# The opening of a two-layer decoder kernel: queues of the first loads, preparation of batches 0 and 1, places of the context projections

## The reference

```python
# x: (8, 256, 128), ctx_1024: (8, 256, 128), all fp32
x = x + self_attention_16_heads(layernorm(x))            # layer 0, heads of 8 columns, W_qkv, W_out
x = x + attention_1_head(layernorm(x), ctx_1024)         # layer 0, keys and values from the context
x = x + expert_mlp(layernorm(x))                         # layer 0
x = x + causal_attention_1_head(layernorm(x))            # layer 1
x = x + attention_16_heads(layernorm(x), ctx_1024)       # layer 1
x = x + light_and_routed_heavy_mlp(layernorm(x))         # layer 1, top 128 of 256 tokens
```

## Time and profile before

| | |
|---|---|
| median of the runs | 435.55 us |
| the profiled execution | 432.98 us |
| its span in the profile | 431.2 us |
| busy: TensorE, VectorE, ScalarE, GpSimd | 357.8, 323.7, 262.1, 141.9 us |

### The profile page before, as it was taken

The page is one execution under the profiler, slowest core; times in us unless marked ns, Lnnn a source line. Parts: engine busy times, 40 slices in busy tenths (PEclk is TensorE's granted clock), DMA queues, the critical chain, the costliest instruction groups (busy, mean ns, idle before and its releaser), DMA issues.

```text
span 431.2 us, 9413 instructions
## 1 busy us (share of the span) xinstructions
PE 357.8 (83%) x3164; PEld 208.3 (48%) x3164; DVE 323.7 (75%) x929; ACT 262.1 (61%) x582; POOL 141.9 (33%) x223
## 2 busy tenths in 40 slices
PE   2454899999999969599987589999989888769793
PEld 1342544454544348469976423444444443326583
DVE  5331888999899346725795687989999994489996
ACT  2130688888888835566554306887878788655531
POOL 3550555446400001301233432456654222221111
PEclk9985999999999997999998956999999999969987
DMA  6213124222360000000000231221221100000003
GB/s 193 74 51 98 45 73 110 76 64 57 106 179 3 2 0 2 2 2 0 2 0 2 74 100 48 51 64 46 70 64 45 45 2 3 0 0 2 0 2 97
DMA packets 36260, 19.98 MB, mean 46 GB/s; under 512 B 4038, under 2 KB 35318, under 8 KB 36214
## 3 DMA queue, kind: packets, MB, share of 16 engines
q1 hardware_dynamic: 35894, 19.25, 16.7%
q10 hardware_dynamic: 320, 0.13, 0.1%
HBM read 5.58 MB, written 1.05 MB: 15 GB/s over the span
## 4 chain that ended last, share of the span: by engine, by line
PE 43%; DVE 33%; ACT 7%; issue 6%; POOL 5%; SPq 3%; DMA 2%; DVEq 0%; ACTq 0%; POOLq 0%
DVE negmax_sb L785 13%; PE pv_ps L1188 10%; PE s_ps L1142 9%; DVE late_sb L1015 5%; PE prep_ps L1098 3%; SPq L405 3%; ACT probT_sb L521 3%; PE s_ps L1238 3%; PE prep_ps L1102 2%; PE s_ps L1151 2%; PE out_ps L1270 2%; POOL rstd_sb L445 2%; PE s_ps L1287 2%; DVE xn_sb L762 2%; PE s_ps L1253 1%
## 5 line engine op out<-in xcount | busy, mean ns | idle before, releaser
L785 DVE TENSOR_REDUCE negmax_sb<-s_ps 128x2 bf16<-128x512 f32 x256 | 162.4, 688 | 35.9 <-PE s_ps L1151 35.8
L521 ACT ACTIVATE probT_sb<-s_ps 128x512 f32<-128x512 f32 x256 | 142.2, 597 | 29.9 <-PE s_ps L1142 27.8
L1151 PE MATMUL s_ps<-stack_sb 62*128 62x256 bf16 x512 | 93.6, 288 | 3.5 <-DMA stack_sb<-parts_sb 3.1
L1142 PE MATMUL s_ps<-stack_sb 63*128 63x256 bf16 x512 | 90.3, 276 | 7.1 <-ACT probT_sb L521 3.2
L1188 PE MATMUL pv_ps<-probT_sb,v_aug_sb 128*32 128x256 f32 x1024 | 69.4, 389 | 0.8 <-ACT probT_sb L521 0.8
L1142 PEld LDWEIGHTS s_ps<-stack_sb 63*128 63x128 bf16 x512 | 30.3, 94 | 65.6 <-ACT probT_sb L521 40.3
L443 POOL TENSOR_SCALAR rstd_sb<-mv_sb 128x2 f32<-128x2 f32 x32 | 7.1, 222 | 124.6 <-DVE mv_sb L754 124.5
L543 ACT ACTIVATE qkf_sb<-prep_ps,b_qkv_sb 128x256 f32<-128x256 f32 x56 | 23.9, 470 | 26.7 <-PE prep_ps L1102 19.7
L1188 PEld LDWEIGHTS pv_ps<-probT_sb,v_aug_sb 128*32 128x32 f32 x1024 | 26.9, 110 | 25.8 <-issue 13.7
L1151 PEld LDWEIGHTS s_ps<-stack_sb 62*128 62x128 bf16 x512 | 30.6, 96 | 11.6 <-DVE negmax_sb L785 6.4
L845 DVE SCALAR_TENSOR_TENSOR x_all_sb<-out_ps,den_inv_sb,x_all_sb 128x128 f32<-128x128 f32 x32 | 9.8, 346 | 25.1 <-PE out_ps L1270 24.9
(11 more groups left out here) (177 smaller groups left out, 659.6 us busy)
## 6 DMA issues: line engine op xcount, KB each, us to landing
stack_sb<-parts_sb SPq DMA_DIRECT2D x192, 64.0 KB, 2.1
x_all_sb<-x SPq DMA_DIRECT2D x4, 256.0 KB, 3.5
ctxT_sb<-ctxT SPq DMA_DIRECT2D x2, 512.0 KB, 5.0
f_w_sb<-f_w SPq DMA_DIRECT2D x2, 512.0 KB, 4.0
out<-x_all_sb SPq DMA_DIRECT2D x4, 256.0 KB, 2.4
d_w_sb<-d_w SPq DMA_DIRECT2D x2, 320.0 KB, 3.6
w_att_sb<-w_att SPq DMA_DIRECT2D x2, 256.0 KB, 3.8
b_vo_sb<-b_vo SPq DMA_DIRECT2D x1, 512.0 KB, 4.9
```

What stands on the lines that cost most here:

```text
L521: act.activation(probT[:, c % 8], s2_ps[c % 2][:, :, :], ACT.Exp, scale=DH ** -0.5).then_inc(exp_ready, 1)
L785: dve.tensor_reduce(negmax[:, n % 2, :, max_column(max_head(h))], s1_ps[c % 3][:, :, :], axis=AX.X, op=ALU.max, negate=True).then_inc(max_ ...
L1142: i = pe.matmul(s2_ps[c % 2][:, k, :], stack[rows, s3, 1, h // 2, k * P:(k + 1) * P], stack[rows, s3, 0, h // 2, :], start=True, stop=True)
L1151: i = pe.matmul(s1_ps[c % 3][:, k, :], stack[rows, s3, 0, hp, k * P:(k + 1) * P], stack[rows, s3, 1, hp, :], start=True, stop=True)
```

## The change

- ScalarE's queue issues both halves of the context, behind a wait for the first quarter of x. SyncE's queue has neither.
- `b_vo` is loaded in two parts: its first layer early, under `w_in`; the other three after the stack fills, under a semaphore of their own, on which GpSimd's first `v_ctx_bias` waits. The second `w_att` and the second quarter of x come ahead of the fills, and all three fills stand before the stack of batch 0.
- Layer norm of batch 1 is computed beside that of batch 0 in step -3, and GpSimd clears stacks 1 and 2 right after their two `rstd_step_`.
- The six key copies of batch 0 are issued on GpSimd's queue (`load_first_keys`), under a semaphore of their own; SyncE issues the six query copies. Who waits for the stack of batch 0 waits for both.
- The split of batch 1 is done by VectorE, at head 9 of step -2 (`FIRST`).
- Of the context projections three run at head 15 of step -2 and five in step -1, after heads 1, 4, 7, 10 and 13.

```diff
@@ -62,9 +62,9 @@
 TOP = 80.0
 LN2 = float(np.log(2.0))
 
-KV_AT = {-2: (8, 14), -1: (0, 2, 4, 10, 12, 14)}
-
-FIRST = (0, B)
+KV_AT = {-2: (15, 15, 15), -1: (1, 4, 7, 10, 13)}
+
+FIRST = (0, 1, B)
 
 UP_AT = (2, 5, 8, 12, 14)
 AHEAD = 2
@@ -207,7 +207,7 @@
         prep_bf = prep_ps[:, :, :].bitcast(bf16)
 
         x_in = [sem(f"x_in{i}") for i in range(4)]
-        w_in, w_cross_in, w_rest_in = sem("w_in"), sem("w_cross_in"), sem("w_rest_in")
+        w_in, w_cross_in, w_rest_in, b_rest_in = sem("w_in"), sem("w_cross_in"), sem("w_rest_in"), sem("b_rest_in")
         ctx_in = [sem(f"ctx_in{i}") for i in range(2)]
         kv_psum, kv_copied, v_ctx_ready = sem("kv_psum"), sem("kv_copied"), sem("v_ctx_ready")
         ones_ready, stack_clear = sem("ones_ready"), sem("stack_clear")
@@ -219,7 +219,7 @@
         part1_ready, rest_ready, parts_ready = sem("part1_ready"), sem("rest_ready"), sem("parts_ready")
         v_psum, v_ready = sem("v_psum"), sem("v_ready")
         bv_ready, fold_psum, bias_folded = sem("bv_ready"), sem("fold_psum"), sem("bias_folded")
-        stacked = [sem(f"stacked{i}") for i in range(3)]
+        stacked, first_keys = [sem(f"stacked{i}") for i in range(3)], sem("first_keys")
         s1_psum, max_ready, maxT_psum, maxT_ready = sem("s1_psum"), sem("max_ready"), sem("maxT_psum"), sem("maxT_ready")
         max_in = [[sem(f"max_in{i}{hf}") for hf in range(2)] for i in range(3)]
         s2_psum, exp_ready, pv_psum, uT_ready = sem("s2_psum"), sem("exp_ready"), sem("pv_psum"), sem("uT_ready")
@@ -254,6 +254,12 @@
         block = ctx.enter_context(nc.Block())
         MANY = (0, B)
 
+        def wait_stacked(eng, n):
+
+            if n == 0:
+                eng.wait_ge(first_keys, STACKED // 2)
+            eng.wait_ge(stacked[n % 3], STACKED * (n // 3 + 1) - (STACKED // 2 if n % 3 == 0 else 0))
+
         def has(n, lo):
 
             return lo <= n < lo + B
@@ -336,7 +342,7 @@
             if m >= 1:
                 eng.wait_ge(parts_ready, m)
             if m >= 2:
-                eng.wait_ge(stacked[(m - 2) % 3], STACKED * ((m - 2) // 3 + 1))
+                wait_stacked(eng, m - 2)
             eng.tensor_copy(parts[:, u, :, 0, :], qkf[:, u]).then_inc(part1_ready, 1)
             eng.wait_ge(part1_ready, n + 1)
             eng.tensor_tensor(rest[:, :, :], qkf[:, u], parts[:, u, :, 0, :], ALU.subtract).then_inc(rest_ready, 1)
@@ -352,32 +358,30 @@
                 sp.dma_start(x_all[:, tiles, :], t["x"].rearrange("b (t p) d -> p (b t) d", p=P)[:, tiles, :]).then_inc(x_in[c], 16)
 
 
+            def load_b_vo(ls, landed):
+                sp.dma_start(b_vo[:, ls, :, :].rearrange("p l w d -> p (l w d)"),
+                             t["b_vo"][ls].rearrange("l w d -> (l w d)").partition_broadcast(P)).then_inc(landed, 16)
+
             load_x(0)
             sp.dma_start(w_att[:, 0:1, :, :], t["w_att"][0:1].rearrange("l w p d -> p l w d")).then_inc(w_in, 16)
             sp.dma_start(b_qkv[:, :, :], t["b_qkv"]).then_inc(w_in, 16)
-            sp.dma_start(b_vo[:, :, :, :].rearrange("p l w d -> p (l w d)"), t["b_vo"].rearrange("l w d -> (l w d)").partition_broadcast(P)).then_inc(w_in, 16)
+            load_b_vo(slice(0, 1), w_in)
+            sp.dma_start(w_att[:, 1:2, :, :], t["w_att"][1:2].rearrange("l w p d -> p l w d")).then_inc(w_cross_in, 16)
+
             def fill_stack(s3):
 
                 sp.wait_ge(stack_clear, s3 + 1)
                 sp.dma_start(max_rows(s3, 1), one_rows[:, :].unsqueeze(1).broadcast_to([2, HP, S])).then_inc(filled[s3], 16)
 
+            load_x(1)
             sp.wait_ge(ones_ready, 1)
-            fill_stack(0)
-            load_x(1)
-            sp.dma_start(w_att[:, 1:2, :, :], t["w_att"][1:2].rearrange("l w p d -> p l w d")).then_inc(w_cross_in, 16)
-
-            def load_ctx(part):
-                half = slice(part * B * S // 2, (part + 1) * B * S // 2)
-                sp.dma_start(ctxT[:, half], t["ctxT"][:, half]).then_inc(ctx_in[part], 16)
-
-            load_ctx(0)
+            for s3 in range(3):
+                fill_stack(s3)
+            load_b_vo(slice(1, L), b_rest_in)
 
             def load_for_later(i):
 
-                if i == -2:
-                    load_ctx(1)
                 if i in (-2, -1):
-                    fill_stack(i + 3)
                     load_x(i + 4)
                 if i == 0:
                     sp.dma_start(w_att[:, 2:L, :, :], t["w_att"][2:L].rearrange("l w p d -> p l w d")).then_inc(w_rest_in, 16)
@@ -401,7 +405,7 @@
                 if n >= 3:
                     sp.wait_ge(s2_psum, H * (n - 2))
                 for r, (jq, jk) in enumerate(TERMS):
-                    for a, j in ((0, jq), (1, jk)):
+                    for a, j in ((0, jq),) if n == 0 else ((0, jq), (1, jk)):
                         sp.dma_start(stack[r::DH, s3, a], parts[:, u, a, j, :]).then_inc(stacked[s3], 16)
 
             for lo in MANY:
@@ -452,7 +456,15 @@
                 x2 = x_all[:, tiles(n), :]
                 pool.tensor_tensor(x2, x2, b_vo[:, l, 1:2, :].broadcast_to([P, NT, D]), ALU.add).then_inc(biased, 1)
 
+            def load_first_keys():
+
+                pool.wait_ge(parts_ready, 1)
+                for r, (jq, jk) in enumerate(TERMS):
+                    pool.dma_start(stack[r::DH, 0, 1], parts[:, 0, 1, jk, :]).then_inc(first_keys, 16)
+
             def v_ctx_bias(b):
+                if b == 0:
+                    pool.wait_ge(b_rest_in, 16)
                 pool.wait_ge(kv_copied, 2 * b + 2)
                 pool.tensor_tensor(v_ctx[:, b], v_ctx[:, b], b_vo[:, 1, 0:1, :].broadcast_to([P, NT, D]), ALU.add).then_inc(v_ctx_ready, 1)
 
@@ -491,11 +503,15 @@
                         if n == B + 6:
                             f_rstd_step()
                 for n in range(lo, lo + B):
-                    if n < B or n >= B + AHEAD_C:
+                    if n == 0:
+                        rstd_step_(0)
+                        rstd_step_(1)
+                        clear_stack(1)
+                        clear_stack(2)
+                        load_first_keys()
+                    elif 2 <= n < B or n >= B + AHEAD_C:
                         rstd_step_(item(n))
                     add_bias(n)
-                    if n in (0, 1):
-                        clear_stack(n + 1)
                     if lo == B and n >= lo + 5:
                         z_norms(n - lo - 5)
                     if n not in FIRST:
@@ -628,6 +644,14 @@
                     act.wait_ge(f_h_psum, f + 1)
                     act.activation(f_hT[:, f, :], s2_ps[f % 2][:, :, :].rearrange("p t q -> p (t q)"),
                                    ACT.Gelu_apprx_tanh).then_inc(f_h_ready, 1)
+
+            def load_ctx(part):
+                half = slice(part * B * S // 2, (part + 1) * B * S // 2)
+                act.dma_start(ctxT[:, half], t["ctxT"][:, half]).then_inc(ctx_in[part], 16)
+
+            act.wait_ge(x_in[0], 16)
+            load_ctx(0)
+            load_ctx(1)
 
             for lo in MANY:
                 if lo == B:
@@ -681,7 +705,7 @@
                             place_max(i, 1)
                         if h == 3 and x is not None:
                             xnT_copy(x)
-                        if h in KV_AT.get(i, ()):
+                        for _ in range(KV_AT.get(i, ()).count(h)):
                             kv_copy(kv_done)
                             kv_done += 1
                         if h == 7 and x is not None:
@@ -949,12 +973,16 @@
                     for h in range(H):
 
                         ln = x if lo else i + 3
-                        if h == at(lo, 0, 1) and ln is not None:
+                        if h == at(lo, 0, 1) and ln is not None and ln != 1:
                             ln_stats(ln)
+                            if ln == 0:
+                                ln_stats(1)
                         if has(i + 1, lo):
                             row_max(i + 1, h)
-                        if h == 2 and ln is not None:
+                        if h == 2 and ln is not None and ln != 1:
                             ln_apply(ln)
+                            if ln == 0:
+                                ln_apply(1)
                         if h == 3 and i == -3:
                             prepare_v_aug(slice(2, 4), 2)
                         if h == 4 and has(i - 1, lo):
@@ -962,6 +990,8 @@
                         if (i, h) == (-3, 9):
                             split(dve, 0)
                             fold_bias(0)
+                        if (i, h) == (-2, 9):
+                            split(dve, 1)
                         if (i, h) == (B - 1, 9) and lo == 0:
                             fold_bias(1)
                         if h == 15 and has(i - 1, lo):
@@ -1163,7 +1193,7 @@
                         pe.wait_ge(exp_ready, c - 1)
                 if first:
                     if h == 0:
-                        pe.wait_ge(stacked[(n + 1) % 3], STACKED * ((n + 1) // 3 + 1))
```

(1 more changed line is left out.)

## The result

The changed kernel took 420.83 us in the median of four runs (420.10 to 421.76), against 436.24 (four runs, 434.41 to 436.97) for the kernel before on the same chips: ratio 0.965, 95% interval 0.961 to 0.970. The forecast was 421.5 in a range of 417.5 to 429. The profiled execution took 420.17 us.

The account below looks back on a forecast made before the run. The opening was taken as bound by the context load waiting behind batch 1's copies. 1.2 + 11.8 + about 1.5 = 14.5 us, rounded to 14, took 435.55 to 421.5 us in the median, range 417.5 to 429.

Parts of the forecast that it names:

- The bound: Opening, 29 to 38 us: context stuck on SyncE behind batch 1's stack copies; TensorE waits 9.8 us, VectorE 11.8.
- The sum: Batch 0's last row maximum: 1.2 + 11.8 + about 1.5 = 14.5 us earlier, rounded down to 14.
- the earlier start: Batch 0's first row-maximum reduction: at 23.4 us instead of 24.62, a gain of 1.2 us.
- the rest: Up to batch 0's last row maximum: the hole, 11.8 us, and low clock and gaps after it, about 1.5.
- Layer norm together: Batches 0 and 1 in the opening: costs nothing, covered by VectorE's idle time before batch 0's split; uncovered 1.3 us.
- Keys on GpSimd: Batch 0's six key copies: 1.1 us each from 13.0, landed at 21.7; the move itself worth nothing.
- Batch 1 earlier: Batch 1's transpose at 13.2 us, 4.4 earlier; VectorE's split gives its parts at 19.8, 6.1 earlier; half spare.
- Projections' places: Three context projections before the row maxima, after v_project(1): 4.4 us, ending at 22.8; first reduction at 23.4.
- B: Opening: batch 0's keys land late, from 1.3 us a copy on GpSimd; 424.2 us at 1.8, 430 at 2.8; chance 0.20.
- E: GpSimd's first key issues make it slower: gain cancelled at 3.7 us a copy, 440.5 us at 4.5; chance 0.04.
- C: TensorE stays at the low clock through the sixteen heads: 8 us more, 429.5; chance 0.06.
- D: The hole moves: a same-sized wait, for w_att, x or batch 2's stack; within 2.2 us of 435.5; chance 0.04.

Follow-up runs that it names:

- e6: Changed kernel with VectorE's clearing of v_aug moved ahead of its layer norm application to batch 1; 420.81 us median, ratio 0.969 to the kernel before.
- e8: Changed kernel with GpSimd's clearing of stacks 1 and 2 waiting for batch 1's layer norm application; 424.21 us profiled, one run.

## Why the prediction was right, and where it was not

**The bound.** That the context waited behind copies that need batch 1's split, and that nothing later makes up for a late opening: shown by the context alone (12.0 us of 14.2) and by half the context back (10 us lost again).

**The sum.** 14.5 us at the last row maximum, rounded to 14; measured 14.2 in the profile. In the medians 15.4, more than the profiles give, with each kernel's runs spread over 1.7 to 2.6 us. The sum holds two errors that cancelled: the earlier start, put at 1.2, was 2.05, and the rest, put at 11.8 + 1.5, was 12.1. The first reduction came at 22.57, not 23.4 (v and projections from 17.12 to 22.1 instead of 17.35 to 22.8, since the second and third took less than I gave them). The sixteen heads took 12.37 us, not 11.2: I gave the stalls 0.7 us, and in the timeline VectorE stands idle for 0.59, 0.58 and 1.03 us, before heads where a context projection goes together with the transpose of batch 2, its query projection, or the transposed maxima. My sum added TensorE's work up to 10.2 us against VectorE's 11.2 and took the larger; I read the stalls so, that such a sum hides where two long pieces together outlast three filled banks. The rounding down by 0.5 us stands for nothing that was seen. In the profiled execution the gain was 12.8 (419.0 forecast, 420.17 measured), since the clock fell where the sixteen-head sublayer ends.

**Layer norm together, "cost nothing".** This step failed. I named the cover (VectorE idle before the split of batch 0) and checked durations, not what runs beside what: VectorE's application stood 3.0 us longer beside GpSimd's two clearings, the memset behind it was late, and batch 0's split began at 12.24, not 10.51. Parts of batch 0 were ready at 14.7, not 13.0. At the last row maximum this cost nothing in the end (34.89 with the order put right), since TensorE's projections ended later still.

**Keys on GpSimd.** The price was mis-sized: 0.56 us a copy (0.525 the median instruction) against 1.1 taken and a low bound of 0.64. GpSimd was the faster issuer. And the value was wrong, "nothing" against 1.7 us, because of the step before: with parts at 14.7, twelve copies on SyncE let TensorE wait until 23.87. With parts at 13.0 they would have landed at about 22.2, just in time; that is an estimate from this row, and no run has both.

**Batch 1 earlier.** Transposed at 12.96 (13.2 forecast), split at 17.11 (17.3), but done at 20.96, not 19.8, since the subtractions ran beside GpSimd. The spare time took it.

**Projections' places.** The prediction weighed them only together with batch 1's earlier steps, by the time at which three in a row would end, and gave the places themselves no price. Measured, the new places cost 1.1 us in the row maxima.

**Rivals.** B and E fell with the price of 0.56 us a copy. The trap that the Trainium skill (SBUF — State Buffer, the "DVE blocks DMA" trap) warns of did not show: the last two of the six copies were issued beside VectorE's split in 0.53 us each, like those before them, and six took 3.38 us in e6, where VectorE was idle beside them; it was VectorE that lost time. The Trainium skill's rule that issuing from several engines saves only the sequencer's time, usually small beside the transfer (DMA: Bandwidth & Descriptors, Issuing engines are not separate DMA queues), does not fit here in its second half: that time was 1.6 to 1.7 us at the mark. C, the low clock, did not last through the heads; yet the clock does fall for some 3 us just behind them in some executions, which no case of mine had, at 1.3 to 1.5 us. D did not occur as a wait of several us. In small it may have: in three of the eleven profiles with the context on ScalarE's queue, in whole or in part (the context alone, the projections' places back, batch 1's split on GpSimd), TensorE's first query projection waited 0.8 to 1.1 us for the biases to land, and in neither of the kernel before; that the context's bytes held them up was not tested.

## What to carry to other kernels

Look on each DMA queue for a load that depends on nothing standing behind copies that wait for computed data, and take it off that queue first; here this one edit was 85% of a change of many, at the first batch's residual. When an instruction is moved into an engine's idle time, check what the other engine of the pair VectorE and GpSimd does there: two memsets on GpSimd stretched a tensor_scalar on VectorE from 0.3 us to 3.4 to 3.6. Judge edits of 1 to 2 us at marks inside the profile, ahead of the next fall of the clock, and not by the total; and profile the same kernel twice, since such a mark moved by 0.5 us here.

## What the runs showed of the hardware that was not expected

- GpSimd issues a 64 KB copy of 128 rows in 0.525 us (six in 3.37), faster than SyncE's 0.60; its copies landed in 2.4 us against 2.1.
- GpSimd's memset of 128x2048 holds VectorE's tensor_scalar until it ends, and leaves VectorE's memset alone. VectorE's subtractions of two SBUF tiles took 1.09 to 1.21 us instead of 0.69 beside GpSimd's additions of two SBUF tiles and its copies. In e6 the copies were over by then: the subtraction beside the additions took 1.10 us, the one after them 0.68.
- TensorE's granted clock fell to half early in step 0 (between 36 and 45 us) in six of the ten profiles without a hole, for some 3 us in five and some 6 us in one (e8); the changed kernel's first, the context alone, the keys back on SyncE and the clearing before the application are free of it. What the engine did ahead of it does not tell them apart: from 22 to 34 us TensorE was busy 9.96 us in the changed kernel's first profile and 9.97 in its second. Why one execution has it and the next has not stays open: the changed kernel had it once in two.
